# A graph network on one core: ScalarE spreads the bytes of two tiles in one instruction, with four tiles of spread counts, three tiles of staging, and the products 15 pairs behind the counts

## The chip, the cores and the metric

The kernel runs on one core of one Trainium2 chip. The metric is the device time of one execution in microseconds (us), over several runs of the same program. Engines are named as the profile names them: PE is TensorE's matmul, PEld its weight load, DVE is VectorE, ACT is ScalarE, POOL is GpSimd, SP is SyncE, whose queue issues most of the transfers (SPq).

## The reference

What is computed is five steps of a message-passing network with a gated unit, and a layer norm (50,000 edges, 3,125 nodes of 128 features):

```
def step(h, _):
    messages = h[col] @ W_msg.T + b_msg
    agg = segment_sum(messages, row, num_segments=num_nodes)
    gi = agg @ W_ih.T + b_ih
    gh = h @ W_hh.T + b_hh
    r, z = sigmoid(i_r + h_r), sigmoid(i_z + h_z)
    n = tanh(i_n + r * h_n)
    return (1 - z) * n + z * h, None
h, _ = lax.scan(step, x, None, length=5)
x = layernorm(x + h)
```

`row` is src and `col` is dst, and dst is sorted. The nodes are cut into 25 tiles of 128.

## The kernel before

The sum over edges is a product with a matrix of counts A, which holds for each pair of nodes the number of edges between them. The kernel makes A once, in bytes, three to a word, and uses it in all five steps. The change touches the stage in which A is made and, for the first step, used at once. This is the counting stage, from about 28 to 158 us.

**The counting loop.** Each of the 25 tiles has four pairs of groups of edges, so there are 100 pairs, p = 0 to 99 (the last tile's four are half as wide). For each pair:

- DVE makes one-hot rows of the edges, for two pairs at a time (`one_hots`, L1303 and L1310, with small ones at L1263 to L1274), in three buffers.
- PE multiplies them, six matmuls a pair (`count`, L682), into one of two PSUM banks. Since there are two banks, the count of pair p waits until pair p - 2 has been copied out.
- ACT copies the bank to a slot of `stage` (`keep_count`, L974). I call this a keep.
- SP (and POOL for two of eight halves) sends the slot to A with a transfer that folds it into rows of A (L478 on SP, six issues a tile; L536 on POOL, two a tile).

`stage` holds eight pairs, two tiles: at the first pair of tile k the keep waits until tile k - 2 has landed in A.

**The spread and the products of the first step.** The product of step 0 needs the bytes of A as f16. ACT spreads each tile of A in three instructions of 1056, 1056 and 576 columns (`spread_bytes`, L986; a cast below), into one of two tiles of `spread`. PE multiplies them with the messages, `parts` (`wide`, L691): six pieces of 448 columns a tile, j = 0 to 5, two matmuls each. I call a piece a product. Products 0 and 1 need the tile's first cast only, 2 and 3 the second, 4 and 5 the third. The seventh piece of all tiles (`last_leg`, on `late`, which DVE casts at L1337) comes after the counting loop.

**What sets the order.** Each engine runs one program in order. ACT's loop over p does the keep of pair p and then the casts that `casts_until` gives to p; PE's does the count of pair p and then the products that `items_until` gives to p. With SPREAD_AT = 9 and USE_AT = 11, the casts of tile k stand after the keeps of pairs 4k+9, 4k+10 and 4k+11, and the products of tile k stand after the counts of pairs 4k+11 (j = 0), 4k+12 (j = 1, 2), 4k+13 (j = 3) and 4k+14 (j = 4, 5). So a cast stands one to three pairs ahead of its first product: two pairs for the first and the second, three for the third. A tile's first cast waits until the tile has landed in A.

After the loop PE has the rest of the products, then the seventh pieces of 23 tiles, then those of the last two tiles. Then come the gates of step 0 (L750 on) and the four other steps, which use A through `ring` and take no part in the change.

Of the kernel before, what the change touches and what calls it, by code (L numbers as in the profile page):

```python
# [6 lines left out]
ACT = mybir.ActivationFunctionType  # L7
# [3 lines left out]
F16 = mybir.dt.float16  # L11
# [3 lines left out]
P = 128  # L15
# [16 lines left out]
DUP = 2  # L32
LEGS = 7
HOTS = 3
STAGED = 8
LATE = 4
SLOTS = 10
LINE = 32
# [29 lines left out]

REST_AT, W_AT = 1, 4

SPREAD_AT, USE_AT = 9, 11

STORED_TOO = (0, 3)

# [6 lines left out]
def gnn_kernel(nc, x, src, dst, w_msg, b_msg, w_ih, w_hh, b_ih, b_hh, out):  # L81
    N = x.shape[0]
    E = src.shape[0]
    KT = -(-N // P)
    GT = P // GROUP
# [4 lines left out]
    PT = GT // 2  # L90
# [3 lines left out]
    LW = NP // LEGS  # L94
    CW = -(-NP // (PLANES * RANGES * 4)) * 4
    WORDS = RANGES * CW
    WIDE = (LEGS - 1) * LW
# [11 lines left out]
    with ExitStack() as ctx:  # L109
# [3 lines left out]
        def sem(name):  # L113
            return ctx.enter_context(nc.semaphore(name))
# [15 lines left out]
        class Row:  # L130
# [15 lines left out]
        A_bytes = A[:, :, :].rearrange("p k w -> p (k w)").bitcast(U8).rearrange(  # L146
            "p (k w b) -> p k w b", k=KT, b=4)
# [5 lines left out]


        counting = Row(AT_WORK)
        spread = counting.next("spread", [P, 2, WIDE], F16)
        stage = counting.next("stage", [P, STAGED, 2, CW], I32)
        AT_HOTS = counting.offset
        iota_high = counting.next("iota_high", [P, HIGH, DUP], BF16)[:, :, :]
# [148 lines left out]
            sem(n) for n in ("bmsg_scaled", "b_high_made", "b_two_made", "bounds_made", "squares_made", "limits_made"))  # L308
        w_turned, w_kept, x_turned, x_kept = (sem(n) for n in ("w_turned", "w_kept", "x_turned", "x_kept"))
        hots_ready, counted, count_kept = sem("hots_ready"), sem("counted"), sem("count_kept")  # L310
        stored = [sem("stored0"), sem("stored1")]
        stored_too = [sem("stored_too0"), sem("stored_too1")]
        spread_made, spread_used, late_made, late_used = (
            sem(n) for n in ("spread_made", "spread_used", "late_made", "late_used"))
        first_made, kept_by_act, kept_by_dve = (sem(n) for n in ("first_made", "kept_by_act", "kept_by_dve"))
# [42 lines left out]
        def placing(p, side):  # L358

            k, q = divmod(p, PT)  # L360
            row = side * P // 2 + q * GROUP
            return (A[row:row + GROUP, k, :].rearrange("c (r w) -> c r w", r=RANGES),
                    stage[:, p % STAGED, side % len(sides(p)), :])

        def landed(k):

            return 16 * (GT - len(STORED_TOO)) * (k // 2 + 1)

        def landed_too(k):
            return 16 * len(STORED_TOO) * (k // 2 + 1)  # L370


        SPREADS = tuple(segments(0, WIDE))
# [3 lines left out]
        def items_until(p):  # L377
            return max(0, p - USE_AT) * (LEGS - 1) // PT

        CASTS = tuple((k, i) for k in range(KT) for i in range(len(SPREADS)))  # L380

        def casts_until(p):
            k, n = divmod(max(0, p - SPREAD_AT), PT)
            return len(SPREADS) * k + min(n, len(SPREADS))


        EARLY = 8
# [66 lines left out]
        @block.sync  # L454
        def _(sp):
            with nc.allow_non_contiguous_dma(reason="the last edge of each row, 125 numbers"):
                sp.dma_start(ends[0:DR, 0:1], dst_2d[:, DW - 1:DW]).then_inc(ends_in, 16)
            sp.dma_start(edges_dst[0:DR, :], dst_2d).then_inc(edges_in, 16)
            for i in range(X_SOONER - 1):
                nodes, tiles = by_tile(x, y, 4 * i, 4 * i + 4)  # L460
                sp.dma_start(tiles, nodes).then_inc(x_in[i], 16)
            for a, z in ((12, 18), (18, KT - 1)):
                nodes, tiles = by_tile(x, y, a, z)
                sp.dma_start(tiles, nodes).then_inc(x_in[-1], 16)
            sp.wait_ge(tail_zeroed, 1)
            nodes, tile = last_tile(x, y)
            sp.dma_start(tile, nodes).then_inc(x_in[-1], 16)
            sp.dma_start(w_raw[:, 0:3, :], w_ih.rearrange("(g p) h -> p g h", p=P)).then_inc(w_in, 16)
            sp.dma_start(w_raw[:, 3:6, :], w_hh.rearrange("(g p) h -> p g h", p=P)).then_inc(w_in, 16)
            sp.wait_ge(flag_set, 1)  # L470
            fast = sp.value_load(flag, min_val=0, max_val=1)
            with sp.If(fast == 1):
                for p in range(PAIRS):
                    k, q = divmod(p, PT)
                    sp.wait_ge(count_kept, p + 1)
                    for side in range(1 if q in STORED_TOO else 2):
                        to, data = placing(p, side)
                        sp.dma_start(to, data).then_inc(stored[k % 2], 16)  # L478
            with sp.Else():
                sp.dma_start(g_dst[0:DR, :], dst_2d).then_inc(gs_src_in, 16)  # L480
                sp.dma_start(g_src[0:DR, :], src_2d).then_inc(gs_src_in, 16)
                with sp.Fori(0, STEPS) as t:
                    sp.wait_ge(gs_msg_kept, t * MU + (MU + 1))
                    nodes, tiles = by_tile(messages, g_msg, 0, KT - 1)
                    sp.dma_start(nodes, tiles).then_inc(gs_msg_stored, 16)
                    nodes, tile = last_tile(messages, g_msg)
                    sp.dma_start(nodes, tile).then_inc(gs_msg_stored, 16)
                sp.wait_ge(gs_msg_stored, 32 * STEPS + 16)

            for b in range(LEGS):  # L490
                tiles = QUADS[b]
                sp.wait_ge(res_made, RES_DONE[b])
                nodes, places = by_tile(out, y, tiles[0], min(tiles[-1] + 1, KT - 1))
                sp.dma_start(nodes, places).then_inc(out_stored, 16)
            sp.wait_ge(out_stored, 16 * LEGS)

        @block.gpsimd
        def _(pool):
# [33 lines left out]
            with pool.If(fast == 1):  # L532
                for p in range(PAIRS):
                    if p % PT in STORED_TOO:
                        pool.wait_ge(count_kept, p + 1)
                        nc.gpsimd.dma_start(*placing(p, 1)).then_inc(stored_too[p // PT % 2], 16)  # L536

                pool.wait_ge(first_made, LEGS)
                for at_piece in SEQUENCE:
                    if at_piece[2] in BY_ACT:  # L540
                        continue
                    if slot_free(at_piece):
                        pool.wait_ge(*slot_free(at_piece))
                    for to, data in expansions(at_piece):
                        last = nc.gpsimd.tensor_copy(to, data)  # L545
                    last.then_inc(made_by_pool, 1)
# [22 lines left out]
        def _(pe):  # L569
# [103 lines left out]
            with pe.If(fast == 1):  # L673
# [13 lines left out]
                def both_parts(k, bank, moving):  # L687

                    last = 1 if k == KT - 1 else 2
                    for part in range(last):  # L690
                        mm = pe.matmul(PS[:, bank, 0:LW], parts[:, k, part, :], moving, start=(k == 0 and part == 0),  # L691
                                       stop=(k == KT - 1), skip_group_check=True)
                    return mm

                def wide(k, j):
                    if j == 0:
                        pe.wait_ge(parts_ready, k // 2 + 1)
                    if (k, MSG_BANKS_FIRST[0]) == (0, j):
                        pe.wait_ge(parts_ready, UNITS)
                    pe.wait_ge(spread_made, k * len(SPREADS) + SPREAD_FOR[j])  # L700
                    return both_parts(k, j, spread[:, k % 2, j * LW:(j + 1) * LW])

                def last_leg(k):
                    pe.wait_ge(late_made, k + 1)
# [150 lines left out]
        def _(act):  # L855
# [109 lines left out]
            with act.If(fast == 1):  # L965

                def keep_count(p):
                    k, q = divmod(p, PT)
                    if k >= 2 and q == 0:
                        act.wait_ge(stored[k % 2], landed(k - 2))  # L970
                        act.wait_ge(stored_too[k % 2], landed_too(k - 2))
                    act.wait_ge(counted, p + 1)
                    n = len(sides(p))
                    nc.scalar.activation(stage[:, p % STAGED, 0:n, :],  # L974
                                         PS[:, COUNT_BANKS[p % 2], 0:n * CW].rearrange("p (s w) -> p s w", s=n),
                                         ACT.Copy).then_inc(count_kept, 1)

                def spread_bytes(k, i):

                    a, w, z, lo = SPREADS[i]  # L980
                    if i == 0:
                        act.wait_ge(stored[k % 2], landed(k))
                        act.wait_ge(stored_too[k % 2], landed_too(k))
                        if k >= 2:
                            act.wait_ge(spread_used, (LEGS - 1) * (k - 1))
                    nc.scalar.activation(spread[:, k % 2, lo:lo + z - w], A_bytes[:, k, w:z, a], ACT.Copy).then_inc(spread_made, 1)  # L986

                for p in range(PAIRS):
                    keep_count(p)
# [127 lines left out]
        def _(dve):  # L1117
# [179 lines left out]
            with dve.If(fast == 1):  # L1297
# [31 lines left out]

                dve.wait_ge(counted, PAIRS)  # L1330
                for k in range(KT):
                    dve.wait_ge(stored[k % 2], landed(k))
                    dve.wait_ge(stored_too[k % 2], landed_too(k))
                    if k >= LATE:
                        dve.wait_ge(late_used, k - LATE + 1)
                    a, w, z, lo = segments(WIDE, NP)[0]
                    nc.vector.tensor_copy(late[:, k % LATE, :], A_bytes[:, k, w:z, a]).then_inc(late_made, 1)  # L1337
# [142 lines left out]
```

## Time and profile before

| | |
|---|---|
| median of 3 runs | 623.12 us (622.49 to 625.57) |
| the profiled execution | 622.44 us, span 620.6 us |
| mean granted clock of TensorE | 0.981 of full speed |
| PE busy over the span | 578.1 us (93%) |
| DVE, ACT, POOL busy | 54%, 52%, 46% |
| the casts L986, 75 instructions | 71.3 us |
| the keeps L974, 100 instructions | 36.9 us |
| the counts L682, 588 matmuls | 52.9 us |
| transfers of stage to A, 200 issues of 66.0 KB | median 3.4 us (SP), 3.5 us (POOL) from issue to landing |

The shares are means over stages with different limits; PE's 93% comes mostly from the four later steps. What the change is worth is read in the counting stage.

### The profile page before, as it was taken

To read this page: it belongs to the slowest core of one execution; us is meant where nothing else is said; L and a number is where in the kernel's file an instruction comes from. 1 tells how busy PE (TensorE), PEld (TensorE's weight loads), DVE (VectorE), ACT (ScalarE), POOL (GpSimd) and SP (SyncE) were. 2 spreads that over 40 slices of the span, in tenths; PEclk is the share of its full clock that TensorE was granted. 3 is DMA by queue.
4 is the path that set the end of the run, shared out by engine and by line. 5 is a ranking of instruction groups with operands and counts; after the bars stand their busy time and mean duration, and the time that the engine had idled before them with its cause. 6 is when DMAs were issued, how large, how long until landed. Compare 5 with 4: busy or idle time off the path is not lost.

```text
span 620.6 us, 8547 instructions
## 1 busy us (share of the span) xinstructions
PE 578.1 (93%) x3090; PEld 330.3 (53%) x3090; DVE 334.0 (54%) x626; ACT 321.2 (52%) x574; POOL 285.2 (46%) x398
## 2 busy tenths in 40 slices
PE   4699999888998999999999999999999999999991
PEld 3575666554555555556555555655555654555550
DVE  5859999975477234336523234732333662354466
ACT  3559998885444444445443335633444444434352
POOL 6012222220302576764567764376566555666600
PEclk9869999999999999999999999999999999999996
DMA  6025668592000000000000000000000000000012
GB/s 171 15 62 124 134 131 122 133 128 46 1 1 1 1 0 1 0 1 0 2 2 0 1 0 1 1 0 1 1 2 0 2 1 0 1 0 1 2 43 64
DMA packets 32220, 18.55 MB, mean 30 GB/s; under 512 B 4657, under 2 KB 31256, under 8 KB 32176
## 3 DMA queue, kind: packets, MB, share of 16 engines
q1 hardware_dynamic: 29050, 13.91, 11.9%
q0 software_dynamic: 1856, 3.90, 2.8%
q8 instruction: 27, 0.44, 0.3%
q10 hardware_dynamic: 1270, 0.16, 0.2%
q14 instruction: 17, 0.14, 0.1%
HBM read 2.84 MB, written 1.60 MB: 7 GB/s over the span
## 4 chain that ended last, share of the span: by engine, by line
PE 76%; DMA 9%; DVE 7%; ACT 5%; issue 2%; SPq 1%; DVEq 0%; ACTq 0%
PE PS L773 40%; PE PS L750 8%; PE PS L754 8%; DMA A<-stage 8%; PE PS L586 5%; PE PS L761 4%; PE PS L760 4%; PE PS L691 3%; ACT spread L986 2%; PE PS L682 1%; SPq L478 1%; ACT stage L974 1%; DVE y L1184 1%; DMA bmsg<-in_L_gnn_b_msg 1%; DVE parts L1143 1%
## 5 line engine op out<-in xcount | busy, mean ns | idle before, releaser
L545 POOL CAST ring<-A 128x896 f16<-128x896 uint8 (+4 forms) x324 | 249.1, 808 | 197.2 <-PE PS L773 182.9
L773 PE MATMUL PS<-ring,parts 128*128 128x448 f16 x1372 | 270.8, 352 | 2.0 <-DVE parts L1143 2.0
L773 PEld LDWEIGHTS PS<-ring,parts 128*128 128x128 f16 x1372 | 133.6, 98 | 128.2 <-issue 10.7
L1348 DVE SCALAR_TENSOR_TENSOR pre_n<-PS,small,gate_r 128x448 f32<-128x448 f32 x35 | 23.9, 683 | 207.3 <-PE PS L761 207.3
L1037 ACT ACTIVATE ring<-A 128x896 f16<-128x896 uint8 (+4 forms) x144 | 105.8, 773 | 0.1
L1020 ACT ACTIVATE gate_r<-PS,small 128x448 f32<-128x448 f32 x35 | 22.2, 633 | 145.2 <-PE PS L754 145.2
L536 POOL DMA_DIRECT2D A<-stage x50 | 26.5, 531 | 101.8 <-ACT stage L974 101.8
L691 PE MATMUL PS<-spread,parts 128*128 128x448 f16 x294 | 70.6, 352 | 1.2 <-ACT stage L974 0.7
L986 ACT ACTIVATE spread<-A 128x1056 f16<-128x1056 uint8 (+1 forms) x75 | 71.3, 956 | 0.6 <-DMA A<-stage 0.6
L682 PE MATMUL PS<-hot_row,hot_key 128*128 128x132 bf16 x588 | 52.9, 227 | 12.9 <-ACT stage L974 7.8
L682 PEld LDWEIGHTS PS<-hot_row,hot_key 128*128 128x128 bf16 x588 | 46.1, 127 | 33.4 <-ACT stage L974 18.8
L750 PE MATMUL PS<-hT,wT 128*128 128x448 f32 x140 | 58.6, 541 | 0.0
L1303 DVE TENSOR_TENSOR hot_key<-iota_key,keyT 128x1536 bf16<-128x1536 bf16 x50 | 47.4, 948 | 2.5 <-PE PS L682 1.3
L974 ACT ACTIVATE stage<-PS 128x264 int32<-128x264 f32 (+1 forms) x100 | 36.9, 387 | 21.7 <-PE PS L682 11.3
L754 PE MATMUL PS<-agg,wT 128*128 128x448 f32 x112 | 46.7, 539 | 0.0
L586 PE MATMUL PS<-wT,hT 128*128 128x128 f32 (+1 forms) x260 | 43.2, 301 | 1.7 <-DVE msg L1131 1.7
L586 PEld LDWEIGHTS PS<-wT,hT 128*128 128x128 f32 (+1 forms) x260 | 38.3, 203 | 10.9 <-issue 6.9
L1030 ACT ACTIVATE cand<-pre_n,small 128x448 f32<-128x448 f32 x35 | 23.4, 668 | 39.5 <-DVE pre_n L1351 39.5
L1310 DVE TENSOR_TENSOR hot_row<-hot_high,hot_low 128x1320 bf16<-128x1320 bf16 x50 | 41.7, 835 | 0.0
L1355 DVE TENSOR_TENSOR pre_n<-hT,cand 128x448 f32<-128x448 f32 x35 | 27.6, 788 | 23.1 <-ACT cand L1030 22.9
L904 ACT ACTIVATE parts<-msg 128x256 f16<-128x256 f32 x48 | 19.5, 414 | 36.8 <-DVE msg L1131 36.8
L1360 DVE TENSOR_TENSOR pre_n<-gate_z,pre_n 128x448 f32<-128x448 f32 x35 | 35.4, 1011 | 1.1
(148 smaller groups left out, 492.7 us busy)
## 6 DMA issues: line engine op xcount, KB each, us to landing
A<-stage SPq DMA_DIRECT2D x150, 66.0 KB, 3.4
A<-stage POOLq DMA_DIRECT2D x50, 66.0 KB, 3.5
y<-in_x SPq DMA_DIRECT2D x3, 256.0 KB, 6.2
y<-in_x SPq DMA_DIRECT2D x2, 384.0 KB
out<-y SPq DMA_DIRECT2D x4, 192.0 KB, 2.2
out<-y SPq DMA_DIRECT2D x3, 256.0 KB, 2.2
edges_dst<-in_dst SPq DMA_DIRECT2D x1, 195.3 KB
w_raw<-in_L_gnn_W_ih SPq DMA_DIRECT2D x1, 192.0 KB
```

The lines of the kernel that those rows point to most:

```text
L545: last = nc.gpsimd.tensor_copy(to, data)
L586: mm = pe.matmul(PS[side * n:(side + 1) * n, msg_bank(t, u), k % 2 * H:(k % 2 + 1) * H], hT[:, k * P:k * P + n], wT[:, 6, :], start=t > 0, ...
L682: mm = pe.matmul(PS[:, COUNT_BANKS[p % 2], side * CW:(side + 1) * CW], hot_key[:, slot, p % 2, :, 3 * side + n], hot_row[:, slot, p % 2, c ...
L691: mm = pe.matmul(PS[:, bank, 0:LW], parts[:, k, part, :], moving, start=(k == 0 and part == 0), stop=(k == KT - 1), skip_group_check=True)
L750: pe.matmul(PS[:, bank, 0:LW], wT[:, 3 + g, :], hb, start=True, stop=False)
L754: mm = pe.matmul(PS[:, bank, 0:LW], wT[:, g, :], gb, start=False, stop=True)
L773: mm = pe.matmul(PS[:, AGG_BANKS[(t * LEGS + b) % 2], 0:LW], parts[:, k, part, :], ring[:, SLOT_OF[at_piece] % SLOTS, k % 2, :], start=(k ...
L974: nc.scalar.activation(stage[:, p % STAGED, 0:n, :], PS[:, COUNT_BANKS[p % 2], 0:n * CW].rearrange("p (s w) -> p s w", s=n), ACT.Copy).the ...
L986: nc.scalar.activation(spread[:, k % 2, lo:lo + z - w], A_bytes[:, k, w:z, a], ACT.Copy).then_inc(spread_made, 1)
L1037: last = nc.scalar.activation(to, data, ACT.Copy)
L1303: nc.vector.tensor_tensor(hot_key[:, d % HOTS, :, :, :], iota_key.unsqueeze(1).to_broadcast([P, 2, P, KEYS]), keyT[:, 2 * d:2 * d + 2, :]. ...
L1310: nc.vector.tensor_tensor(hot_row[:, d % HOTS, :, :, :].rearrange("p h c (a b d) -> p (h c) a b d", a=HIGH, d=DUP), highs.unsqueeze(3).to_ ...
```

## The change

A cast takes two tiles in one instruction (only the last tile, the 25th, is alone). `spread` has four tiles and `stage` three tiles of pairs, with semaphores for each of the three. The casts begin at pair 13 and the products at pair 15. Line numbers after it are one to four higher.

```diff
-STAGED = 8
+STAGED = 12
...
-SPREAD_AT, USE_AT = 9, 11
+SPREAD_AT, USE_AT = 13, 15
...
-        spread = counting.next("spread", [P, 2, WIDE], F16)
+        spread = counting.next("spread", [P, 4, WIDE], F16)
...
-        CASTS = tuple((k, i) for k in range(KT) for i in range(len(SPREADS)))
+
+        CASTS = tuple((k, i) for k in range(0, KT, 2) for i in range(len(SPREADS)))
 
         def casts_until(p):
-            k, n = divmod(max(0, p - SPREAD_AT), PT)
-            return len(SPREADS) * k + min(n, len(SPREADS))
+            k, n = divmod(max(0, p - SPREAD_AT), 2 * PT)
+            return len(SPREADS) * k + min((n + 1) // 2, len(SPREADS))
...
-                    pe.wait_ge(spread_made, k * len(SPREADS) + SPREAD_FOR[j])
-                    return both_parts(k, j, spread[:, k % 2, j * LW:(j + 1) * LW])
+                    pe.wait_ge(spread_made, k // 2 * len(SPREADS) + SPREAD_FOR[j])
+                    return both_parts(k, j, spread[:, k % 4, j * LW:(j + 1) * LW])
...
-                    if k >= 2 and q == 0:
-                        act.wait_ge(stored[k % 2], landed(k - 2))
-                        act.wait_ge(stored_too[k % 2], landed_too(k - 2))
+                    if k >= len(stored) and q == 0:
+                        act.wait_ge(stored[k % len(stored)], landed(k - len(stored)))
+                        act.wait_ge(stored_too[k % len(stored)], landed_too(k - len(stored)))
...
                     a, w, z, lo = SPREADS[i]
+                    n = min(2, KT - k)
                     if i == 0:
-                        act.wait_ge(stored[k % 2], landed(k))
-                        act.wait_ge(stored_too[k % 2], landed_too(k))
-                        if k >= 2:
-                            act.wait_ge(spread_used, (LEGS - 1) * (k - 1))
-                    nc.scalar.activation(spread[:, k % 2, lo:lo + z - w], A_bytes[:, k, w:z, a], ACT.Copy).then_inc(spread_made, 1)
+                        for tile in range(k, k + n):
+                            act.wait_ge(stored[tile % len(stored)], landed(tile))
+                            act.wait_ge(stored_too[tile % len(stored)], landed_too(tile))
+                        if k >= 4:
+                            act.wait_ge(spread_used, (LEGS - 1) * (k - 4 + n))
+                    nc.scalar.activation(spread[:, k % 4:k % 4 + n, lo:lo + z - w], A_bytes[:, k:k + n, w:z, a],
+                                         ACT.Copy).then_inc(spread_made, 1)
```

ACT's program, where the casts begin. Before, from the keep of pair 9 on (`stage` is a keep, `spread` a cast):

```order
L974 ACTIVATE stage<-PS 128x264
L986 ACTIVATE spread<-A 128x1056
L974 ACTIVATE stage<-PS 128x264
L986 ACTIVATE spread<-A 128x1056
L974 ACTIVATE stage<-PS 128x264
L986 ACTIVATE spread<-A 128x576
L974 ACTIVATE stage<-PS 128x264 x2
```

The same place now, the five keeps being those of pairs 9 to 13:

```order
L975 ACTIVATE stage<-PS 128x264 x5
L989 ACTIVATE spread<-A 128x2x1056
L975 ACTIVATE stage<-PS 128x264 x2
L989 ACTIVATE spread<-A 128x2x1056
L975 ACTIVATE stage<-PS 128x264 x2
L989 ACTIVATE spread<-A 128x2x576
L975 ACTIVATE stage<-PS 128x264 x4
```

For tiles k and k+1 (k even) the casts now stand after the keeps of pairs 4k+13, 4k+15 and 4k+17. For tile k the second is one pair ahead of product 2, which stands after the count of pair 4k+16, and the third is one pair ahead of product 4 (pair 4k+18); both were two and three pairs ahead. The first stays two pairs ahead.

PE's program at the end of the counting loop, before (the counts of the last tile have three matmuls; `late` is the seventh piece):

```order
L682 MATMUL PS<-hot_row,hot_key 128x132 x3
L691 MATMUL PS<-spread,parts 128x448 x12
L691 MATMUL PS<-late,parts 128x448 x46
L691 MATMUL PS<-spread,parts 128x448 x12
L691 MATMUL PS<-late,parts 128x448 x2
```

And now:

```order
L683 MATMUL PS<-hot_row,hot_key 128x132 x3
L692 MATMUL PS<-spread,parts 128x448 x24
L692 MATMUL PS<-late,parts 128x448 x46
L692 MATMUL PS<-spread,parts 128x448 x12
L692 MATMUL PS<-late,parts 128x448 x2
```

Six more products, twelve matmuls, have moved behind the last count, and those of tile 22 now need a cast that waits for tile 23.

## Rows read from the trace of the kernel before

**Rows 1.** Busy time by stretch: us, PE, PEld, DVE, ACT, POOL, then clock

```profile
53.00:143.00 90.00, 81.13 (x755) 53.95 (x752) 82.34 (x147) 79.80 (x151) 22.22 (x42) 1.00 0.77 130
143.00:158.00 15.00, 14.80 (x78) 7.58 (x79) 9.32 (x25) 7.13 (x11) 0.53 (x1) 1.00 0.10 23
```

**Rows 2.** Waits from 46 to 143 us: total, times, longest

```profile
ACT stage L974 <- DMA A<-stage: 9.8, 14, 2.5
PE PS L682 <- ACT stage L974: 7.8, 10, 2.5
...
PEld PS L691 <- ACT spread L986: 3.1, 16, 0.3
```

**Rows 3.** The chain that ended last, 26 to 160 us: start, us, what

```profile
56.05 0.04 issue
...
60.90 0.61 SPq L478
...
130.18 10.20 DMA A<-stage x2
...
143.20 14.74 PE PS L691 x77
```

**Rows 4.** DVE in order of time, three of its rows: start, us

```profile
49.05 0.84 DVE L1310 TENSOR_TENSOR hot_row<-hot_high,hot_low 128x1320 bf16<-128x1320 bf16 x1
...
56.06 0.95 DVE L1303 TENSOR_TENSOR hot_key<-iota_key,keyT 128x1536 bf16<-128x1536 bf16 x1
...
59.99 0.95 DVE L1303 TENSOR_TENSOR hot_key<-iota_key,keyT 128x1536 bf16<-128x1536 bf16 x1
```

**Rows 5.** SP's issues from 51.6 to 139.6 us, merged, and landing times of L478

```profile
51.62 87.89 SPq L478 DMA_DIRECT2D A<-stage  x126
...
DMA to landing us min/median/max: 2.4/3.4/6.3
```

**Rows 6.** ACT in order of time, keeps and casts

```profile
67.85 1.09 ACT L986 ACTIVATE spread<-A 128x1056 f16<-128x1056 uint8 x1
68.82 0.39 ACT L974 ACTIVATE stage<-PS 128x264 int32<-128x264 f32 x1
69.09 1.09 ACT L986 ACTIVATE spread<-A 128x1056 f16<-128x1056 uint8 x1
...
112.77 0.70 ACT L986 ACTIVATE spread<-A 128x576 f16<-128x576 uint8 x1
113.34 0.75 ACT L974 ACTIVATE stage<-PS 128x264 int32<-128x264 f32 x2
```

**Rows 7.** PE in order of time: a count after a wait, products, a count

```profile
79.86 0.55 PE L682 MATMUL PS<-hot_row,hot_key 128*128 128x132 bf16 x6 [0.20 <-ACT stage L974]
80.25 0.92 PE L691 MATMUL PS<-spread,parts 128*128 128x448 f16 x4
81.01 0.51 PE L682 MATMUL PS<-hot_row,hot_key 128*128 128x132 bf16 x6
81.36 0.54 PE L691 MATMUL PS<-spread,parts 128*128 128x448 f16 x2
```

**Rows 8.** A cast on ACT, and PE's weight load for the product that waits for it

```profile
89.23 1.09 ACT L986 ACTIVATE spread<-A 128x1056 f16<-128x1056 uint8 x1
...
90.38 0.20 PEld L691 LDWEIGHTS PS<-spread,parts 128*128 128x128 f16 x2 [0.18 <-ACT spread L986]
```

**Rows 9.** Casts of two tiles' bytes to `ring` in the later steps, by form

```profile
L1037 ACT ACTIVATE ring<-A 128x896 f16<-128x896 uint8 x80 | 74.3, 939 | 0.1
```

**Rows 10.** ACT after the last keep: the casts of tile 23

```profile
143.92 2.63 ACT L986 ACTIVATE spread<-A 128x1056 f16<-128x1056 uint8 x3 [0.21 <-DMA A<-stage]
```

**Rows 11.** Busy time and granted clock (third number from the end) before the loop

```profile
24.00:26.00 2.00, 0.54 (x12) 0.31 (x11) 1.27 (x5) 0.83 (x4) 0.00 (x0) 1.00 0.00 0
26.00:28.00 2.00, 0.00 (x0) 0.00 (x0) 1.55 (x2) 0.00 (x0) 0.00 (x0) 0.67 0.02 8
28.00:40.00 12.00, 11.62 (x61) 9.25 (x62) 6.69 (x15) 6.14 (x14) 1.16 (x2) 0.50 0.18 46
```

More of the change, by code:

```diff
@@ L310, in gnn_kernel @@
         hots_ready, counted, count_kept = sem("hots_ready"), sem("counted"), sem("count_kept")
-        stored = [sem("stored0"), sem("stored1")]
-        stored_too = [sem("stored_too0"), sem("stored_too1")]
+        stored = [sem(f"stored{i}") for i in range(STAGED // PT)]
+        stored_too = [sem(f"stored_too{i}") for i in range(STAGED // PT)]
         spread_made, spread_used, late_made, late_used = (
@@ L365, in landed @@
         def landed(k):
-            return 16 * (GT - len(STORED_TOO)) * (k // 2 + 1)
+            return 16 * (GT - len(STORED_TOO)) * (k // len(stored) + 1)
         def landed_too(k):
-            return 16 * len(STORED_TOO) * (k // 2 + 1)
+            return 16 * len(STORED_TOO) * (k // len(stored) + 1)
         SPREADS = tuple(segments(0, WIDE))
@@ L477, in _ @@
                         to, data = placing(p, side)
-                        sp.dma_start(to, data).then_inc(stored[k % 2], 16)
+                        sp.dma_start(to, data).then_inc(stored[k % len(stored)], 16)
             with sp.Else():
@@ L535, in _ @@
                         pool.wait_ge(count_kept, p + 1)
-                        nc.gpsimd.dma_start(*placing(p, 1)).then_inc(stored_too[p // PT % 2], 16)
+                        nc.gpsimd.dma_start(*placing(p, 1)).then_inc(stored_too[p // PT % len(stored)], 16)
                 pool.wait_ge(first_made, LEGS)
@@ L1331, in _ @@
                 for k in range(KT):
-                    dve.wait_ge(stored[k % 2], landed(k))
-                    dve.wait_ge(stored_too[k % 2], landed_too(k))
+                    dve.wait_ge(stored[k % len(stored)], landed(k))
+                    dve.wait_ge(stored_too[k % len(stored)], landed_too(k))
                     if k >= LATE:
```

## The prediction

> **What bounds the kernel now.** I read the busy time by stretch first. The later steps are PE's alone and the change doesn't reach them, so they can only be shifted: whatever the change does, it does before 157.94 us, where the products of step 0 end [rows 3]. From 53 to 143 us three engines stand close together: PE 81.1, DVE 82.3 and ACT 79.8 us busy of 90 [rows 1]. No one of them is far behind the limit, so the order in which they hand work to each other matters as much as their loads.
>
> The waits of that stretch come next: ACT's keeps wait 9.8 us in 14 places for the transfers of `stage`, and PE's counts wait 7.8 us for ACT's keeps [rows 2]. They are one chain: a late landing holds a keep, which holds a PSUM bank, which holds a count. The chain of the end says the same (10.20 us of two transfers from 130.18 on, then 14.74 us of products without a gap from 143.20) [rows 3]. Behind the transfers stands SP's queue: a single issue takes 0.61 us [rows 3], six a tile, and 126 of them fill 87.89 us, 0.70 apiece and 4.2 us a tile, with landing 3.4 us later in the median and up to 6.3 [rows 5]. DVE, left alone, needs 3.93 us a tile (the same instruction of the next tile at 56.06 and 59.99) [rows 4]. So the loop now runs at 8.2 to 8.4 us for two tiles, DVE's 7.87 plus what SP adds late in the loop.
>
> The smallest row is the one to look at: the products' weight loads wait for ACT's casts 16 times, 3.1 us in all, never over 0.3 [rows 2]. The cast ends just as PE comes to it: at 89.23 + 1.09 = 90.32, and the load starts at 90.38 [rows 8]. Two pairs' distance was only just enough for a cast of 1.09 us.
>
> **The change, part by part.**
>
> *Three tiles of staging.* The keep of tile k waits for tile k-3, one tile (some 4 us) later than now; the 9.8 us of waits go as long as SP keeps up. Nothing is added. Alone it could give back at most what separates the loop from DVE's pace.
>
> *A cast of two tiles.* Start to next start, a cast of 1056 columns takes 0.97 (67.85 to 68.82) and one of 576 takes 0.57 (112.77 to 113.34) [rows 6], so 0.83 ns a column and 0.09 us for the instruction. Two tiles then take 1.85 and 1.05 us; twice the single ones, 1.94 and 1.14, is the upper bound. A dearer two-tile form is not to be expected, since ACT casts 2 x 448 columns of the same A in 0.94 us later in the kernel [rows 9], where the line through the single ones gives 0.95 from start to end. I take 1.85 and 1.05. 37 instructions fewer save ACT 37 x 0.09 = 3.3 us.
>
> The Trainium skill's page Advanced Engine Details and Errata (The Read-Write Bubble) advises large tiles for ScalarE, to pay the gap between instructions less often. The trace agrees with the gap, 0.09 us; by that rule alone the sum would be 3.3 us less, and by the rows below it would be some 23 us more.
>
> *The distances.* The second and third cast now stand one pair ahead of their first product, at nearly twice the length. I follow two tiles, eight pairs, through both engines. From PE's rows a count takes 0.35 (0.39 after a wait), one product 0.38, two 0.76, and a count's result is there 0.16 after the next instruction may start (0.51 against 0.35) [rows 7]; so is a cast's result 0.12 later than its successor's start, with 0.05 to PE's load [rows 6, 8], together 0.16; a keep takes 0.27 on ACT (68.82 to 69.09) [rows 6], and it follows its count by 0.04, as a count follows a keep (56.05) [rows 3].
>
> Start when ACT has done the keep of pair 4k+15.
> 1. Second cast 1.85, hand-over 0.16. PE, meanwhile, has done one product, count 4k+16 and product 1, some 0.7 us, and stands before product 2: it waits 1.3 us. Behind this product stand all later counts. Product 2 (0.38) and count 4k+17 (0.35 + 0.16 + 0.04) follow. ACT needs that count for its next keep but one, 0.27. Sum 3.21.
> 2. Third cast 1.05 + 0.16; PE waits again, now before product 4. Products 4 and 5 and count 4k+19: 0.76 + 0.35. Sum 5.53.
> 3. PE goes on without a wait: product, count, two products, count of 4k+21: 0.38 + 0.35 + 0.76 + 0.35. Sum 7.37.
> 4. 0.20, the keep of 4k+21 (0.27), the next first cast 1.85, and the keeps of 4k+22 and 4k+23, which stand behind it (0.54). Sum 10.23.
>
> Each engine waits for the other in turn: PE has 7.4 us of work in it, ACT 4.75 + 8 x 0.27 = 6.9, and two PSUM banks let PE run no further ahead. So two tiles take **10.24 us**, 5.1 a tile, against DVE's 3.93 and SP's 3.9 to 4.2. The transfers fall out of the chain: their limit is 7.7 us from a tile's last keep to the cast that wants it (six pairs at 1.28), above the longest landing, 6.3 [rows 5].
>
> *The sum over the loop.* The one-hots of pairs 12 and 13 are ready at 49.05 + 0.84 = 49.89 [rows 4]. Two counts, a keep and the first cast (0.35 + 0.35 + 0.20 + 0.27 + 1.85) give 52.95, two keeps 53.5, the second cast with hand-over 55.5: the first product held starts there. Tile 20's like it comes ten rounds later, at 157.9. Then the rest of that round, with half-size counts: 0.38 + 0.38, keep 0.17, cast 1.05 + 0.16, 0.76, and the last count and keep, 0.6: ACT and PE are through with pair 99 at 161.4.
>
> *The tail.* PE has 11 more products to do there, of which six of tile 22, whose cast stands behind the last keep: 1.85 + 1.85 + 1.05 + 0.16 and its two last products 0.76 give 167.0. Then 23 seventh pieces, six products, one piece at 0.378 each (11.3) and seven single matmuls at 0.189 (1.3), all from 77 matmuls in 14.74 less its few gaps [rows 3]: **179.7 us**. Restarts after a wait cost 0.03 to 0.04 each (0.39 against 0.35), three a round and ten rounds: 1.0. End of the products: 180.7 against 157.94, **22.7 us later**. What follows is the same work, and begins from the same last product.
>
> The profiled execution took 622.44 us and the median of three is 623.12, 0.7 above it. 622.44 + 22.7 is 645.1; on the median, **645.8 us**.
>
> **The rivals.**
>
> *The lag holds and batching pays (faster).* ACT's fewer starts, 3.3 us, and its 9.8 us of waits are what the loop wants, and PE doesn't meet the casts. For that a two-tile cast must be over before PE is at product 2, 0.7 us after it starts; it takes 1.85 by rows 6 and 9. Were it so, the loop would be DVE's and SP's, and the end would hang on tile 23's landing, now 143.9 [rows 10]. SP without its long issues (126 x 0.64 = 80.6 of 87.9) would bring that to about 137, and the casts and tail behind it, 18.3 less the 4.5 that are then hidden, end at 151 to 158: 615 to 622 us. This is also the case that the skill's rule on large tiles points to.
>
> *The landing stays the limit.* The products wait less than I think, say because ACT runs ahead elsewhere, and only the tail is longer: tile 22's casts now wait for tile 23, landed at 142.8 to 143.9, + 4.9 + 0.8 + 12.6 = 161.1 to 162.2, 3.2 to 4.3 us more: 626 to 627 us. Against it: the waits follow from order and durations alone.
>
> *The clock falls.* PE has only counts until pair 15, from 47 to 53 us: about 0.5 busy every 1 us. Before the loop its clock went to half (1.2 GHz) at 26.7 us, after a stretch of 0.54 busy in 2 us, and at 0.5 it stayed over 12 us of nearly full work [rows 11]. If the sparse counts do this again, two tiles take 14.7 us (8 counts and 12 products at double length, 0.70 and 0.76, all PE's) for as long: up to 12 x (1 - 10.24/14.7) = 3.6 us more, 646 to 650 us. In the rounds themselves PE is busy 72% of the time, with gaps of 1.3 us at most; I don't expect it there.
>
> The Trainium skill (TensorE: Matmul & The Clock Gate, architectural detail on the array) says that ScalarE's queue is strictly first in, first out. If keeps could pass a waiting cast the rounds would be shorter; no row shows one out of order.
>
> **How the numbers follow.** Rounds of 10.24 with full clock 0.74; clock fallen for a while 0.14; rounds shorter than reckoned, between 628 and 640, 0.04; the landing as limit 0.04; faster 0.04. The time is that of the first. Its own errors: 0.94 of the cast's length against twice the single (10.24 to 10.6 a round, up to +3.5), hand-overs of 0.1 more or less three times a round (3 us either way). Low 640.5: hand-overs and restarts better, and a hidden piece; high 650: dearer casts, or the clock. A change of 0.5% (3 us) is about what a measurement here can tell: faster 0.04, same 0.02, slower 0.94.
>
> **What would show it.** Right: cast rows of about 1.95 and 1.16 us; products waiting for casts some 20 times over a microsecond (second cast) and 0.9 us (third), 20 to 25 us in all; ACT's keeps waiting for counts; no wait for landings; DVE idle over 2 us in a round; SP idle between issues; the first cast of each two tiles 10.2 to 10.4 us after the last one; products' end at 180 to 181. Wrong: a cast much shorter than 1.9, rounds at 8 us, keeps that wait for transfers, or a clock below 1.00 in the loop.

## The result, and the profile after

The changed kernel takes 646.75 us in the median of 4 runs (645.62 to 647.32), against 622.81 (622.49 to 625.57) for the kernel before beside it: a ratio of 1.0376, 95% interval 1.034 to 1.0412, slower by 24 us. The prediction was 645.8, in a range from 640.5 to 650.

The profiled execution after has a span of 645.0 us, 24.4 more than before. ACT in order of time shows one round of two tiles (start us, us):

```profile
63.44 1.96 ACT L989 ACTIVATE spread<-A 128x2112 f16<-128x2112 uint8 x1
65.29 0.66 ACT L975 ACTIVATE stage<-PS 128x264 int32<-128x264 f32 x2
65.83 1.97 ACT L989 ACTIVATE spread<-A 128x2112 f16<-128x2112 uint8 x1
67.69 0.40 ACT L975 ACTIVATE stage<-PS 128x264 int32<-128x264 f32 x1
68.80 0.39 ACT L975 ACTIVATE stage<-PS 128x264 int32<-128x264 f32 x1 [0.71 <-PE PS L683]
69.09 1.16 ACT L989 ACTIVATE spread<-A 128x1152 f16<-128x1152 uint8 x1
70.14 0.38 ACT L975 ACTIVATE stage<-PS 128x264 int32<-128x264 f32 x1
71.61 0.39 ACT L975 ACTIVATE stage<-PS 128x264 int32<-128x264 f32 x1 [1.09 <-PE PS L683]
72.42 0.39 ACT L975 ACTIVATE stage<-PS 128x264 int32<-128x264 f32 x1 [0.42 <-PE PS L683]
73.45 0.39 ACT L975 ACTIVATE stage<-PS 128x264 int32<-128x264 f32 x1 [0.63 <-PE PS L683]
73.74 1.96 ACT L989 ACTIVATE spread<-A 128x2112 f16<-128x2112 uint8 x1
```

From first cast to first cast it is 73.74 - 63.44 = 10.30 us, and ACT stands still four times in it, 2.85 us in all, each time for a count. PE's side of the same round:

```profile
65.54 0.54 PE L692 MATMUL PS<-spread,parts 128*128 128x448 f16 x2 [0.59 <-ACT spread L989]
65.91 0.51 PE L683 MATMUL PS<-hot_row,hot_key 128*128 128x132 bf16 x6
66.26 0.54 PE L692 MATMUL PS<-spread,parts 128*128 128x448 f16 x2
67.86 0.55 PE L692 MATMUL PS<-spread,parts 128*128 128x448 f16 x2 [1.06 <-ACT spread L989]
68.25 0.51 PE L683 MATMUL PS<-hot_row,hot_key 128*128 128x132 bf16 x6
...
70.30 0.93 PE L692 MATMUL PS<-spread,parts 128*128 128x448 f16 x4 [0.81 <-ACT spread L989]
```

The second cast ends at 65.83 + 1.97 = 67.80 and the product behind it starts at 67.86. The count of the next pair (68.25) comes only then, and ACT's keep of it at 68.80: each engine waits for the other, as the eight pairs were followed in the prediction. The chain that ended last goes through the same places (start us, us, what):

```profile
65.95 1.86 ACT spread L989
...
67.86 0.55 PE PS L692 x2
...
69.19 1.06 ACT spread L989
...
70.30 0.93 PE PS L692 x4
...
73.74 1.96 ACT spread L989
```

It changes from ACT's cast to PE's products twice in a round, at the second and at the third cast. The waits of the stretch, with their total, number and longest, from 46 to 165 us:

```profile
ACT stage L975 <- PE PS L683: 34.8, 47, 1.6
PE PS L692 <- ACT spread L989: 25.6, 32, 1.2
...
DVE hot_key L1307 <- PE PS L683: 21.0, 19, 1.3
```

Before, the products' weight loads waited 3.1 us for casts and ACT's keeps 9.8 us for transfers [rows 2]. After, no wait for a transfer is left in this stretch, and DVE, which set the pace with SP, is held for 21 us. A transfer also lands sooner: the last number is the median in us from issue to landing, and it was 3.4 before.

```profile
A<-stage SPq DMA_DIRECT2D x150, 66.0 KB, 2.6
```

The tail, PE after the last count:

```profile
163.66 3.39 PE L692 MATMUL PS<-spread,parts 128*128 128x448 f16 x16
167.89 1.98 PE L692 MATMUL PS<-spread,parts 128*128 128x448 f16 x8 [0.84 <-ACT spread L989]
169.71 8.87 PE L692 MATMUL PS<-late,parts 128*128 128x448 f16 x46
...
182.48 1.77 PE L751 MATMUL PS<-hT,wT 128*128 128x448 f32 x4
```

and the gates' first row in the kernel before:

```profile
157.87 1.77 PE L750 MATMUL PS<-hT,wT 128*128 128x448 f32 x4
```

The gates start at 182.48 instead of 157.87: 24.6 us later, where the span has grown by 24.4.

### The profile page after: what moved, and what is told of

Its sections match the earlier page's. It is cut to its first block, busy times and chain, and to the rows that moved or that the text cites. A ratio compares the mean times of both kernels' runs of the same rounds, so it can differ in the third digit from the quotient of the medians.

```text
span 645.0 us, 8510 instructions
## 1 busy us (share of the span) xinstructions
PE 583.2 (90%) x3090; PEld 334.0 (52%) x3090; DVE 336.0 (52%) x626; ACT 320.3 (50%) x538; POOL 285.1 (44%) x398
## 4 chain that ended last, share of the span: by engine, by line
PE 78%; ACT 12%; DVE 7%; issue 1%; DMA 1%; ACTq 0%; DVEq 0%
PE PS L774 38%; ACT spread L989 8%; PE PS L751 8%; PE PS L755 8%; PE PS L692 7%; PE PS L587 5%; PE PS L762 4%; PE PS L761 4%; PE PS L683 3%; ACT stage L975 2%; DVE y L1188 1%; DMA bmsg<-in_L_gnn_b_msg 1%; DVE hot_key L1307 1%; DVE parts L1147 1%; DVE hot_row L1314 1%
## 5 line engine op out<-in xcount | busy, mean ns | idle before, releaser
L692 PE MATMUL PS<-spread,parts 128*128 128x448 f16 x294 | 73.8, 359 | 26.6 <-ACT spread L989 26.5
L1024 ACT ACTIVATE gate_r<-PS,small 128x448 f32<-128x448 f32 x35 | 22.2, 634 | 145.2 <-PE PS L755 145.2
L989 ACT ACTIVATE spread<-A 128x2112 f16<-128x2112 uint8 (+3 forms) x39 | 63.3, 1636 | 0.0
L683 PEld LDWEIGHTS PS<-hot_row,hot_key 128*128 128x128 bf16 x588 | 49.6, 128 | 20.9 <-DVE hot_row L1314 3.8
L1307 DVE TENSOR_TENSOR hot_key<-iota_key,keyT 128x1536 bf16<-128x1536 bf16 x50 | 47.8, 955 | 22.2 <-PE PS L683 21.0
L692 PEld LDWEIGHTS PS<-spread,parts 128*128 128x128 f16 x294 | 23.6, 98 | 45.0 <-ACT spread L989 27.4
```

What stands on the lines that cost most here:

```text
L683: mm = pe.matmul(PS[:, COUNT_BANKS[p % 2], side * CW:(side + 1) * CW], hot_key[:, slot, p % 2, :, 3 * side + n], hot_row[:, slot, p % 2, c ...
L989: nc.scalar.activation(spread[:, k % 4:k % 4 + n, lo:lo + z - w], A_bytes[:, k:k + n, w:z, a], ACT.Copy).then_inc(spread_made, 1)
L1307: nc.vector.tensor_tensor(hot_key[:, d % HOTS, :, :, :], iota_key.unsqueeze(1).to_broadcast([P, 2, P, KEYS]), keyT[:, 2 * d:2 * d + 2, :]. ...
```

## The experiments

Eleven more kernels were run. Ratios are to runs of the kernel before beside them on the same chip, whose median was 621.48 us for four of them and 623.44 for the others; the interval is the 95% one.

**Products one pair later.**

```diff
-SPREAD_AT, USE_AT = 13, 15
+SPREAD_AT, USE_AT = 13, 16
```

> The changed kernel with the products of the first step one pair later (USE_AT = 16 for 15), and nothing else. Theory A (distance: PE stands before products 2 and 4 because their casts are one pair ahead, and the counts are queued behind them): the second cast is then two pairs ahead, the waits all but go, two tiles take some 8.1 to 8.6 us for 10.3, and the time falls by 15 to 19 us, to 628 to 632 us; what stays above 622.8 is the longer tail after the last count. Rival B (the casts as such: a long instruction on ACT holds back the keeps, wherever the products stand): rounds of over 9.5 us and over 640 us. Rival C (staging, memory or the clock): no change, 645 to 648.

631.31 us, ratio 1.0135 (1.0055 to 1.0216), within theory A's 628 to 632. One number takes back 15 of 24 us; the four runs lie wide apart, from 627.5 to 634.7. ACT's first casts of two rounds:

```profile
67.90 1.96 ACT L989 ACTIVATE spread<-A 128x2112 f16<-128x2112 uint8 x1
...
76.27 1.96 ACT L989 ACTIVATE spread<-A 128x2112 f16<-128x2112 uint8 x1
```

8.37 us a round for 10.30, with the same instructions on each engine and the same length of a cast. (Seven of the nine rounds are so; two take 8.8, where the first cast waits 0.4 us for products that still use its place in `spread`.) The products' waits for casts have fallen from 25.6 us in 32 places:

```profile
PE PS L692 <- ACT spread L989: 8.8, 12, 3.5
```

So the casts as such (rival B) don't cost the time, their place before the products does. Theory A holds. The gates start at 165.26 in this execution, 17.2 us sooner than in the changed kernel. Nine rounds give 16.4 of it (92.70 less 76.26). The first round gives 1.4. The first cast stands 2.5 us earlier, at 49.89, 1.9 of them because DVE is that much ahead in this execution. The end takes 3.1 us more, since the first cast behind the last keep waits 4.4 us for its transfers.

**Two instructions in place of one.**

```diff
-                    nc.scalar.activation(spread[:, k % 4:k % 4 + n, lo:lo + z - w], A_bytes[:, k:k + n, w:z, a],
-                                         ACT.Copy).then_inc(spread_made, 1)
+                    for tile in range(k, k + n):
+                        last = nc.scalar.activation(spread[:, tile % 4, lo:lo + z - w], A_bytes[:, tile, w:z, a], ACT.Copy)
+                    last.then_inc(spread_made, 1)
```

> The changed kernel with each two-tile cast issued as two single-tile casts one after the other at the same place, the semaphore raised by the second. Theory A: what costs is that ACT is held for 1.9 us at this place and the product waits for the end of it; two instructions cost 0.09 more per cast, 0.27 us a round, so the rounds go from 10.30 to 10.55 and the time to 649 to 650. Rival B (the two-tile form of the instruction itself is what costs, by its access pattern): the time falls clearly below 645.

650.81 us, ratio 1.0449 (1.0385 to 1.0513). The round, by its first casts:

```profile
72.78 2.05 ACT L990 ACTIVATE spread<-A 128x1056 f16<-128x1056 uint8 x2
...
83.35 1.08 ACT L990 ACTIVATE spread<-A 128x1056 f16<-128x1056 uint8 x1
```

(The second row is cut short by the end of the view; there are two casts there as well.) The round is 10.57 us, 0.27 more than with one instruction: three times 0.09, as reckoned. The two-tile form is not dear. It saves 0.27 us a round, while the products of the changed kernel wait 2.46 us a round for the casts (0.59, 1.06 and 0.81 above). The time is 0.8 us above the 649 to 650 expected, and its interval overlaps that of the changed kernel; the 0.27 is read from the rounds.

**Single casts at the old distances, three tiles of staging.**

```diff
-SPREAD_AT, USE_AT = 13, 15
+SPREAD_AT, USE_AT = 9, 11
-        CASTS = tuple((k, i) for k in range(0, KT, 2) for i in range(len(SPREADS)))
+        CASTS = tuple((k, i) for k in range(KT) for i in range(len(SPREADS)))
-            k, n = divmod(max(0, p - SPREAD_AT), 2 * PT)
-            return len(SPREADS) * k + min((n + 1) // 2, len(SPREADS))
+            k, n = divmod(max(0, p - SPREAD_AT), PT)
+            return len(SPREADS) * k + min(n, len(SPREADS))
-                    n = min(2, KT - k)
+                    n = 1
```

and the products' wait for `k * len(SPREADS)` casts again.

> The changed kernel with single-tile casts at the old places and the products at the old distance (SPREAD_AT = 9, USE_AT = 11), keeping three tiles of staging and four of spread counts. Theory A: the 24 us go; what staging is worth alone is small, since SP's issues (126 in 87.9 us before) set the late part of the loop: 621.5 to 623 us. Rival B (the waits of 9.8 us for the transfers were the loop's limit, so that a third tile of staging gives them back): 614 to 618. Rival C (the larger tiles in memory cost): above 630.

621.8 us, ratio 0.9979 (0.9948 to 1.0011): no difference that can be told, and within theory A's 621.5 to 623. The larger tiles in memory cost nothing that can be told, and a third tile of staging is worth little. Its waits for landings have moved (46 to 165 us):

```profile
ACT spread L989 <- DMA A<-stage: 7.8, 13, 1.4
```

Where the keeps waited 9.8 us for tile k-2 [rows 2], now the first casts wait 7.8 us in all, each for its own tile. A third tile moved the wait and didn't remove it. That SP's lateness is behind it is shown by the runs with POOL's third transfer below.

**The changed kernel with two tiles of staging.**

```diff
-STAGED = 12
+STAGED = 8
```

> The changed kernel with two tiles of staging (STAGED = 8 for 12). Theory A: in rounds of 10.3 us the transfers land long before a keep wants the slot, so the third tile is worth nothing here: within 1 us of 646.8. Rival B (staging carries part of the time, and hides a loss of the other edits): 650 or more, with keeps waiting for landings.

645.31 us, ratio 1.0365 (1.0301 to 1.0429), as the changed kernel's 1.0376. The median is 1.4 us below the changed kernel's, a little more than the 1 us expected, and the intervals overlap. The third tile has no part in the 24 us that can be told.

**The kernel before with its products one pair earlier.**

```diff
-SPREAD_AT, USE_AT = 9, 11
+SPREAD_AT, USE_AT = 9, 10
```

> The kernel before with its products one pair earlier (USE_AT = 10 for 11), so that single-tile casts stand one pair ahead of the products, as the second one does in the changed kernel. Theory A (distance and length of the cast together): the wait before product 2 of each tile is about 0.2 to 0.4 us with a cast of 1.09, and PE has little slack to lose it in: 1 to 5 us slower than before, 624 to 628. Rival B (distance alone, whatever the length): some 20 us slower. Rival D (the distance has nothing to do with it): no change.

625.29 us, ratio 1.007 (1.0053 to 1.0087): 4.4 us slower by the ratio, as theory A said. Its waits, 46 to 143 us:

```profile
PE PS L691 <- ACT spread L986: 8.8, 20, 0.4
```

Products wait 20 times for casts of 1.09 us, 0.4 us each. At the same distance of one pair they waited 1.06 us for a cast of 1.96 us and 0.81 for one of 1.16, and even two pairs ahead 0.59 for one of 1.96. Distance and length belong together.

**Two-tile casts sooner.** The casts after pairs 4k+13, 4k+14 and 4k+16, so that each stands two pairs ahead of its first product:

```diff
-            return len(SPREADS) * k + min((n + 1) // 2, len(SPREADS))
+            return len(SPREADS) * k + sum(n > at for at in (0, 1, 3))
```

> The changed kernel with its two-tile casts after pairs 4k+13, 4k+14 and 4k+16 (they stood at 13, 15 and 17), the products where they were, so that each cast stands two pairs ahead of its first product. Theory A, followed through the same durations: the waits before products 2 and 4 shrink, but the first two casts now have a single keep between them, which holds back the counts; two tiles take about 9.2 us for 10.3, 636 to 640 us. Rival B (only the number of pairs between cast and product matters): as with the products one pair later, 8.4 us and 628 to 632.

633.22 us, ratio 1.0167 (1.0123 to 1.0211). Its round, by the first casts:

```profile
70.27 1.96 ACT L989 ACTIVATE spread<-A 128x2112 f16<-128x2112 uint8 x1
72.13 0.38 ACT L975 ACTIVATE stage<-PS 128x264 int32<-128x264 f32 x1
72.40 1.97 ACT L989 ACTIVATE spread<-A 128x2112 f16<-128x2112 uint8 x1
...
79.47 1.96 ACT L989 ACTIVATE spread<-A 128x2112 f16<-128x2112 uint8 x1
```

9.20 us, as followed through; the time was missed by 3 us, it came below the 636 to 640. The rule "two pairs ahead" alone (8.4) is wrong. The reason is not the one in the expectation, that the keep between two casts holds back the counts: in the waits from 46 to 165 us no matmul of a count waits for a keep. It is a product that still waits, in the same round:

```profile
74.42 0.55 PE L692 MATMUL PS<-spread,parts 128*128 128x448 f16 x2 [0.78 <-ACT spread L989]
```

The two long casts stand nearly together, so the second ends 2.1 us after the first (72.23 and 74.37), and PE has no more to do between them than a product, a count and a product.

**PE busy before its first product.** The matmuls of the counts of pairs 8 to 14 are issued three times.

```diff
-                        for n, c in enumerate(COLS_OF[side]):
+                        for n, c in tuple(enumerate(COLS_OF[side])) * (3 if 8 <= p < 15 else 1):
```

> The changed kernel with the matmuls of the counts of pairs 8 to 14 issued three times (each repeat starts its sum anew, so the counts stay the same), to keep PE busy before its first product. Theory A (in the changed kernel the granted clock fell to half from about 50 to 58 us, since PE had only counts there, and the first round took 11.07 us for 10.30): the clock stays at 1.00 there, the first round takes 10.3, and the time falls by 0.5 to 1.5 us, to 645 to 646.3. Rival B (the repeats cost what the clock gives, or the clock falls whatever PE does): no change, or up to 2 us slower.

648.28 us, ratio 1.045 (1.0432 to 1.0467). The clock did stay up, but no time came of it: the kernel is slower than the changed one (1.0376, 1.034 to 1.0412), by 1.5 us between the medians and by more between the ratios. Busy time by stretch (us, PE, PEld, DVE, ACT, POOL, granted clock, DMA share, GB/s), the changed kernel first:

```profile
46.00:53.00 7.00, 4.55 (x45) 3.65 (x46) 6.94 (x14) 3.30 (x9) 1.98 (x4) 0.70 0.41 106
53.00:57.00 4.00, 3.68 (x22) 2.13 (x21) 4.00 (x8) 4.00 (x5) 0.53 (x1) 0.50 0.50 122
...
58.00:59.00 1.00, 1.00 (x7) 0.56 (x6) 1.00 (x4) 0.58 (x2) 0.00 (x0) 0.50 0.51 135
59.00:60.00 1.00, 0.48 (x7) 0.35 (x6) 1.00 (x2) 1.00 (x2) 0.00 (x0) 1.00 0.00 0
```

and with the repeated counts:

```profile
46.00:53.00 7.00, 7.00 (x117) 6.77 (x118) 6.30 (x12) 2.48 (x8) 1.43 (x3) 1.00 0.35 92
53.00:57.00 4.00, 2.56 (x33) 1.84 (x30) 4.00 (x8) 4.00 (x5) 0.68 (x2) 1.00 0.36 95
```

Its first round took 10.37 us (first casts at 53.20 and 63.57) against 11.07 in the changed kernel (52.37 and 63.44), but it began 0.83 us later: the repeats kept PE busy for the whole 7.00 us up to 53. That they cost what the clock gave fits these rows. The expectation of the time failed; that of the clock held. By the last round the two kernels are level (last first casts at 156.25 and 156.14), so the trace shows no more than the 0.4 us between the spans; where the rest of the difference between the ratios comes from is open. What the fallen clock costs the changed kernel can only be estimated from its rows: 0.8 us in the first round (11.07 less 10.30), and about as much before it, where the counts that the first cast stands behind ran at half clock.

**SP's queue.** In the kernel before, POOL takes three of a tile's eight transfers:

```diff
-STORED_TOO = (0, 3)
+STORED_TOO = (0, 1, 3)
```

> The kernel before with POOL issuing three of a tile's eight transfers instead of two, so that SP has five (STORED_TOO = (0, 1, 3)). Theory A (SP's issues, 0.70 us each with the long ones, six a tile, are what makes the late part of the loop slower than DVE's 3.93 a tile): five a tile take 3.2 to 3.5 us, landings come earlier, and the time falls by 2 to 5 us, to 618 to 621. Rival B (the transfers themselves, or the DMA engines, are the limit): no change within 1.5 us.

616.39 us, ratio 0.9938 (0.9921 to 0.9955): 3.9 us faster by the ratio, within the 2 to 5 expected, though the time itself is below the 618 to 621. Its products run without a gap from 136.42 us (143.20 before [rows 3]):

```profile
136.42 14.74 PE PS L691 x77
```

These 6.8 us overstate it: the first cast of this execution already stands at 45.94 us, 2.2 sooner than the 48.13 of the kernel before, since the clock came back sooner (1.00 from 32 to 36 us, where it was 0.50 before). From the first cast of tile 0 to that of tile 21 it takes 83.20 us against 86.62, 3.96 a tile against 4.12, where DVE alone needs 3.93. The keeps' waits for landings are 9.8 us no longer:

```profile
ACT stage L974 <- DMA A<-stage: 3.7, 4, 1.3
```

A transfer takes no less time from issue to landing than before (3.7 us in the median, 3.4 before), so it is SP's issues, and not the transfers themselves (rival B), that were the limit of the loop's late part. The same with three tiles of staging and single casts:

```diff
-STORED_TOO = (0, 3)
+STORED_TOO = (0, 1, 3)
```

> Single-tile casts at the old distances, three tiles of staging and four of spread counts, and POOL issuing three of eight transfers. Theory A: the loop is DVE's, 3.93 us a tile, keeps no longer wait for landings, 617 to 620; the third tile of staging adds nothing to POOL's third issue, or 1 us. Rival B (staging was worth more than SP's queue let through): 614 to 616.

616.21 us, ratio 0.9928 (0.9906 to 0.9951), between theory A's 617 to 620 and rival B's 614 to 616. Beside POOL's third transfer, staging adds nothing that can be told. And with four of eight:

```diff
-STORED_TOO = (0, 1, 3)
+STORED_TOO = (0, 1, 2, 3)
```

> Single-tile casts, three tiles of staging, and POOL issuing four of a tile's eight transfers. Theory A: with three the loop is already DVE's, 3.93 us a tile, so a fourth changes nothing: within 1 us of 616.2. Rival B (SP was still the limit with three): 613 to 615.

614.62 us, ratio 0.988 (0.9828 to 0.9931). That lies in rival B's 613 to 615 and not in theory A's, but the interval overlaps that of three transfers. In the traces the rounds are DVE's with three and with four, as theory A said: 82.67 and 82.66 us from the first cast of tile 0 to that of tile 21, 3.94 a tile. From there to the gates it takes 22.2 us with three and 20.6 with four, of which 1.5 us are a wait of tile 22's first cast for its landing that is gone with four. Whether that is a gain from run to run these intervals can't tell. It is the lowest median run here, and faster than both kernels.

**Both remedies on two-tile casts.** Products at 16, POOL with three of eight (the two edits above, on the changed kernel).

> The changed kernel with the products at pair 16 and POOL issuing three of a tile's eight transfers. Theory A: ACT and PE still set the rounds at about 8.2 to 8.4 us, so SP's relief gives at most 2 us of the 631.3 with products at 16: 627 to 631, and two-tile casts stay slower than the kernel before. Rival B (what is left above the kernel before is SP's): 622 to 625.

625.99 us, ratio 1.0049 (1.0028 to 1.0069), 1 us below theory A's range and 1 above rival B's. Between the medians the relief of SP gave 5.3 us where 2 were expected, but the 631.31 is that of runs from 627.5 to 634.7. In the two profiled executions it takes 111.8 us from the first cast to the gates (51.80 to 163.58) for 115.4 with six issues (49.89 to 165.26), 3.6 less. The rounds stay at 8.4 (first casts at 95.06 and 103.42 give 8.36); 2.8 of the 3.6 us came at the end, where the casts of tile 22 stand behind tile 23's landing. PE's product that needs them, with SP's six issues and then with five:

```profile
148.35 1.59 PE L692 MATMUL PS<-spread,parts 128*128 128x448 f16 x4 [3.55 <-ACT spread L989]
```

```profile
147.22 0.92 PE L692 MATMUL PS<-spread,parts 128*128 128x448 f16 x4 [1.29 <-ACT spread L989]
```

Two-tile casts stay slower than the kernel before.

## Why the prediction was right

The time came within 1 us of the forecast and the mechanism is the one forecast: PE stands before products 2 and 4, the counts are queued behind them, and ACT waits for the counts. That it is as close as 1 us is partly luck. The span grew by 24.4 us where 22.7 were reckoned; the 0.7 that the forecast adds, because the median before lay above the profiled execution, hid part of this, since after the change the median (646.75) lies just below the profiled 646.89. The steps in the order of the prediction:

- *What bounds the kernel.* Right: DVE and SP set the loop of before. With SP relieved it ran 3.9 us faster, at 3.96 us a tile against DVE's 3.93. Staging alone gives nothing measurable (ratio 0.9979, 0.9948 to 1.0011); that it could give back "at most what separates the loop from DVE's pace" was a bound far above its worth.
- *The cast of two tiles.* 1.85 and 1.05 us from start to start were taken; 63.44 to 65.29 is 1.85 and 69.09 to 70.14 is 1.05. Two instructions instead cost 0.27 a round.
- *The round.* 10.24 us, or 10.34 with restarts, against 10.30 in nine rounds (63.44 to 156.14 us). It fits step by step too: from the second cast's start at 65.83 the four steps end 3.26, 5.59, 7.42 and 10.30 us later, where 3.21, 5.53, 7.37 and 10.23 were reckoned. PE's waits are shorter than named, 1.06 and 0.81 us for 1.3 and 0.9, which the sum doesn't use. One wait was left out of the prose: PE also waits 0.59 us for the first cast. It lies beside ACT's chain in step 4 and doesn't change the sum, but brings the number of waits to 32 where some 20 were named. Their total, 25.6 us, is just above the 20 to 25. DVE's 21.0 us of waits are the 2 us a round that were forecast.
- *The cause.* Theory A is shown by three kernels with the same instructions in other places: 10.30 us a round with distances of 2, 1, 1 pairs, 9.20 with 2, 2, 2 and a single keep between the first two casts, 8.37 with the products one pair later. The split casts, at 10.57, rule out the two-tile form.
- *The tail.* From the last round's first cast to the end of the products: 26.2 us predicted (180.7 less 154.5), 26.3 measured (156.14 to 182.48).
- *What was off.* The end came at 182.5 and not 180.7. The first cast began at 52.37 instead of 51.1: 0.5 us is the start of the loop, which was that much later in this execution, the other 0.8 is what counts at half clock can account for. The first round took 11.07 for 10.3, mostly at half clock (with the repeated counts, at full clock, it took 10.37). The nine other rounds gave 0.4 back, at 10.30 for 10.34.
- *The rivals.* The clock fell, as that rival said (0.70, then 0.50 of full), but only until 59 us. The case given 0.74, full clock throughout, is therefore not what ran, and one of the prediction's own signs of being wrong, a clock below 1.00 in the loop, was there. It decided little: by the two estimates above it cost some 1.5 us and not up to 3.6. In the first round PE still waited for the first cast and the third (0.31 and 0.53 us), so part of its slowness was hidden behind ACT. From 60 us on the clock is at 1.00. The landing as limit is refuted: no wait for a transfer is left in the changed kernel's loop. The Trainium skill's rule on large tiles (Advanced Engine Details and Errata, The Read-Write Bubble) was true in its own sum, 0.27 a round, nine times smaller than the waits that the place of the casts brought.

## What to carry to other kernels

When one instruction takes over the work of two, its consumer waits for the end of the longer one: the distance in the program must grow with its length, or the saving of a start (0.09 us here) buys a wait of a microsecond. Distance counts in time and not in pairs: two pairs were not enough where the two casts stood close together. Where two engines hand buffers back and forth with two banks, follow one whole round through both programs before you change a place, and count what is queued behind the waiting instruction. And a wait on a buffer can be the mark of a late queue elsewhere: a third tile of staging moved the wait (9.8 us for one tile became 7.8 for another), while moving one issue of six to another queue cut it to 3.7 us and brought the loop to DVE's pace.

## What the runs showed of the hardware

Before the loop the granted clock falls to half, and when it comes back differs between executions. Two executions, the kernel before and then the one with single casts and three tiles of staging, which do the same work there:

```profile
26.00:46.00 20.00, 16.33 (x101) 12.81 (x101) 13.10 (x27) 9.54 (x23) 2.21 (x4) 0.66 0.19 49
```

```profile
26.00:46.00 20.00, 14.19 (x115) 11.31 (x115) 14.33 (x28) 9.74 (x25) 2.22 (x4) 0.84 0.21 56
```

The mean clock of the stretch was 0.66 and 0.84, and the second had 14 more matmuls behind it at 46 us (115 for 101). Runs of the kernel before lie between 619.2 and 625.6 us over all chips, and the shorter ones have the higher mean clock: 619.2 us with 0.987 of full speed, 625.4 with 0.974 on the same chip. That this clock makes the spread is likely and was not tested. It also means that a single profile of this kernel can stand 3 us off its median: the second of these took 618.89 us where its median is 621.8.
